# When GpSimd may refill a ring of gathered rows: released by the products that read them, or by the whole first layer behind them

## The chip, the cores and the metric

The kernel runs on one core of one Trainium2 chip. The metric is device time in microseconds (us) of one execution. The names of the engines are those of the profile: PE is TensorE, whose weight loads are told apart as PEld; DVE is VectorE, ACT is ScalarE, POOL is GpSimd, and SP is SyncE, which here only issues DMAs.

## The reference, cut to what matters

The reference is a graph network with 3125 nodes, 50000 edges and four message passing steps. The edges come sorted by their target node.

```
edge_attr = swish(edge_attr_raw @ enc_W + enc_b)                  # 50000 x 128
for _ in range(4):
    e_in = concat([edge_attr, x[src], x[dst]])                    # 50000 x 384
    e_upd = layernorm(swish(e_in @ eW1 + eb1) @ eW2 + eb2) * eg + ebeta
    edge_attr = edge_attr + e_upd
    agg = segment_sum(edge_attr, dst)                             # 3125 x 128
    x = x + layernorm(swish(concat([x, agg]) @ nW1 + nb1) @ nW2 + nb2) * ng + nbeta
return layernorm(x0 + x)
```

## The kernel before, in words

The product of the node features with their two parts of the edge layer's weights is made once per step and node and kept in two tables in DRAM: `p_table` for sources, `q_table` for targets. A row of `p_table` has 512 half-precision numbers (256 hidden units, as a high and a low part). So x[src] @ eW1 becomes a gather of rows of `p_table`.

Edges are worked on in groups of 512 (four tiles of 128, `TPG = 4`); there are 98 groups (`G1`) in each of the 4 steps. The input's edges are sorted, so every engine's program takes the branch that calls the functions `fast_...`, and there the object `F1` of the class `Edge` with `wide = False` does the edges.

In the pass of group g, PE does in this order (`fast_pe`):
- `hidden(g)`: 4 products with the target rows (L1123); 16 products that add the gathered source rows, four for each tile (L1131), after which it increments the semaphore `src`; then the 6 products of the first layer with the edge's own state (L1139), after which it increments `h`.
- `turn(g + 2)`: 8 transposes (L1103), then the semaphore `transposed`.
- `output(g - 1)`: a bias product (L1150) and the 24 products of the second layer (L1155), then the semaphore `v`.
- `node_sums(g - 7)`: 8 products with the 0/1 matrix of the targets (L1171), then the semaphore `sum`.

ACT waits for `h` to apply Silu (L1242, L1243), copies the transposed state (L1269), and waits for `v` to square the result with a sum (L1257). DVE makes the low half of the activations (L1349), adds the group's sums to `agg` when `sum` has come (L1419), and does the rest of the layer norm.

The gathered rows lie in a ring of four buffers (`R = 4`). POOL does nothing else in an edge step than gather them: for each group four indirect DMAs (L1080), one for each tile. Before the four it waits until the buffer of the group four places back has been read: L1078, a wait on `src`. The first four groups of a step have no such wait. The rest of the order is fixed by the program text; there is no planner. SP's queue loads the state, the matrices and the target rows and stores the new state.

Of the kernel before, what the change touches and what calls it, by code (L numbers as in the profile page):

```python
# [44 lines left out]
R = 4  # L45
# [14 lines left out]
def build_program(nc, x_in, src_in, dst_in, attr_in, enc_W, enc_b, eW1, eb1, eW2, eb2, eg, ebeta,  # L60
                  nW1, nb1, nW2, nb2, ng, nbeta, out):
    ctx = ExitStack()
    with ctx:
# [610 lines left out]
        class Init:  # L674
# [180 lines left out]
            def pool(self, pool):  # L855
                S, here, count = self.S, self.here, self.count

                for g in here:
                    k = g % R
                    pool.wait_ge(S("hi"), count(g))  # L860
                    pool.tensor_tensor(st0[k][:, :, D:2 * D], e0[k].rearrange("p (t f) -> p t f", t=TPG),
                                       st0[k][:, :, 0:D], ALU.subtract).then_inc(S("lo"), 1)
# [62 lines left out]
        class Edge(Groups):  # L925
# [142 lines left out]
            def pool(self, pool, s):  # L1068

                S = self.S  # L1070
                if s and not self.wide:
                    for t in range(CH):
                        pool.wait_ge(ND(f"tab{t}"), 16 * NCH * s)

                def gather(g):
                    k = g % R
                    if g - R >= self.lo:
                        pool.wait_ge(S("src"), s * self.per_step + g - R + 1)  # L1078
                    for t in range(TPG):
                        pool.indirect_dma_start(  # L1080
                            out=rows[k][:, t, :], out_offset=None, in_=p_table,
                            in_offset=bass.IndirectOffsetOnAxis(ap=idx_all[:, g, t:t + 1], axis=0),
                        ).then_inc(self.rows_sem(g), 16)

                for g in range(self.lo, self.hi):
                    gather(g)
# [825 lines left out]
```

## Time and profile before

| | |
|---|---|
| device time, median of 3 runs | 3248.82 us (3248.39 to 3252.28) |
| span of the profiled execution, first to last instruction | 3309.1 us |
| PE busy | 2595.5 us (78%) |
| DVE busy | 2336.3 us (71%) |
| ACT busy | 2083.8 us (63%) |
| POOL busy | 1702.6 us (51%) |
| mean share of the 16 DMA engines, four edge stretches | 0.67, 0.67, 0.66, 0.55 |
| granted TensorE clock there | 1.00 |

Of the profiled execution no other time than its span is given; the span is 60.3 us above the median of the runs without a profile. Busy times are those of records; a matmul's end is modelled, and its start says when it was taken up. "Idle before" in square brackets is how long an engine stood still before the row, and after the arrow stands what ended that; "remote" means that a semaphore came at that moment at which no recorded instruction ended.

### The profile page before, as it was taken

How to read it: one execution, taken by the hardware profiler on the slowest of the kernel's cores; microseconds unless marked ns; L12 is line 12 of the kernel's file. 1: busy time of each engine (PE TensorE's matmuls, PEld its weight loads, DVE VectorE, ACT ScalarE, POOL GpSimd, SP SyncE). 2: the span in 40 equal slices, each digit the busy share in tenths (PEclk: the TensorE clock that was granted, in tenths of full speed). 3: DMA queues.
4: the chain of work that ended last, by engine and by line, in shares of the span. 5: the costliest groups of instructions: out<-in, count | busy, mean ns of one | idle time of the engine just before them, and what ended most of it. 6: DMA issues, size and time to landing. Idle time of an engine off the chain costs nothing.

```text
span 3309.1 us, 86038 instructions
## 1 busy us (share of the span) xinstructions
PE 2595.5 (78%) x28086; PEld 1911.6 (58%) x28086; DVE 2336.3 (71%) x6778; ACT 2083.8 (63%) x5559; POOL 1702.6 (51%) x1679
## 2 busy tenths in 40 slices
PE   3665888888887788888887788888888688888886
PEld 1332666666664566666665566666665466666664
DVE  6884677777784577777786477777776377777777
ACT  3774666666663566666664566666675466666674
POOL 2445566566531556665640666665540665666550
PEclk8656999999999899999999899999999899999998
DMA  4776566666644566666653566666663455555550
GB/s 129 249 248 205 171 196 194 195 200 195 194 149 134 159 194 195 202 196 194 198 166 121 155 198 199 196 195 201 194 182 111 146 158 156 163 156 161 159 149 25
DMA packets 492918, 578.05 MB, mean 175 GB/s; under 512 B 82399, under 2 KB 341724, under 8 KB 492446
## 3 DMA queue, kind: packets, MB, share of 16 engines
q1 hardware_dynamic: 417198, 366.82, 34.8%
q0 software_dynamic: 75264, 205.62, 23.0%
q8 instruction: 228, 3.74, 0.5%
q14 instruction: 228, 1.87, 0.2%
HBM read 428.62 MB, written 144.35 MB: 173 GB/s over the span
## 4 chain that ended last, share of the span: by engine, by line
PE 59%; issue 16%; ACT 6%; DVE 6%; another core or an unknown queue 6%; DMA 3%; SPq 1%; DVEq 1%; POOL 0%; ACTq 0%; POOLq 0%
PE psum L1155 13%; PE psum L1139 13%; PE psum L1131 12%; PE psum L1123 5%; PE psum L1103 5%; PE psum L1171 4%; PE psum L1150 2%; PE psum L1577 2%; PE psum L1616 2%; ACT arena L1269 1%; ACT psum L1243 1%; ACT arena L1257 1%; PE psum L1590 1%; DMA arena<-attr_p 1%
## 5 line engine op out<-in xcount | busy, mean ns | idle before, releaser
L1080 POOL DMA_INDIRECT arena<-node_tables,idx_all x1568 | 1582.0, 1009 | 1342.0 <-PE psum L1131 626.5
L1257 ACT ACTIVATE arena<-psum 128x128 f32<-128x128 f32 x1568 | 411.6, 278 | 741.3 <-remote 723.1
L1131 PE MATMUL psum<-ident,arena 128*128 128x128 f16 x6272 | 548.1, 220 | 410.6 <-issue 398.8
L1131 PEld LDWEIGHTS psum<-ident,arena 128*128 128x128 f16 x6272 | 399.3, 98 | 541.1 <-issue 521.9
L1349 DVE SCALAR_TENSOR_TENSOR arena<-psum,arena 128x1024 f16<-128x1024 f32 x392 | 477.0, 1217 | 202.9 <-issue 146.9
L1155 PE MATMUL psum<-w_hi,arena 128*128 128x128 f16 x6272 | 595.2, 220 | 4.6 <-DVE arena L1349 3.5
L1155 PE MATMUL psum<-w_lo,arena 128*128 128x128 f16 x3136 | 550.5, 220 | 1.2 <-issue 1.2
L1419 DVE TENSOR_TENSOR agg<-agg,psum 128x128 f32 x392 | 113.0, 288 | 569.5 <-remote 544.8
L1242 ACT ACTIVATE arena<-psum 128x1024 f16<-128x1024 f32 x392 | 402.2, 1026 | 172.3 <-remote 75.7
L1155 PEld LDWEIGHTS psum<-w_hi,arena 128*128 128x128 f16 x6272 | 502.2, 98 | 6.8 <-DVE arena L1349 4.7
L1139 PE MATMUL psum<-arena,w_hi 128*128 128x512 f16 x1568 | 479.7, 386 | 29.8 <-issue 29.6
L1385 DVE SCALAR_TENSOR_TENSOR arena<-arena 128x128 f32<-128x128 f32 x1568 | 489.9, 346 | 4.0 <-DVE arena L288 0.4
L1269 ACT COPY arena<-psum 128x1024 f16<-128x1024 f16 x392 | 400.0, 1020 | 45.7 <-remote 22.0
L1243 ACT ACTIVATE psum<-psum 128x1024 f32<-128x1024 f32 x392 | 401.2, 1023 | 0.0
L1155 PEld LDWEIGHTS psum<-w_lo,arena 128*128 128x128 f16 x3136 | 308.8, 98 | 48.3 <-issue 3.5
L1257 ACT ACTIVATION_READ_ACCUMULATOR arena<-psum 128x1 f32 x1568 | 325.8, 208 | 0.0
L1139 PE MATMUL psum<-arena,w_lo 128*128 128x512 f16 x784 | 303.1, 387 | 7.8 <-issue 7.6
L1103 PEld LDWEIGHTS psum<-ident,arena 128*128 128x128 f16 x3136 | 211.5, 100 | 144.1 <-issue 46.6
L1359 DVE TENSOR_TENSOR arena<-psum,g_row 128x512 f32<-128x512 f32 x392 | 266.3, 679 | 30.3 <-ACT arena L1257 27.5
L1396 DVE SCALAR_TENSOR_TENSOR arena<-arena 128x512 f32<-128x512 f32 x392 | 279.2, 712 | 6.7
L1123 PE MATMUL psum<-arena 128*128 128x256 fp8e4 x1568 | 253.0, 274 | 36.3 <-issue 23.2
L1103 PE MATMUL psum<-ident,arena 128*128 128x128 f16 x3136 | 245.5, 222 | 41.4 <-DMA arena<-state 18.2
(172 smaller groups left out, 3514.9 us busy)
## 6 DMA issues: line engine op xcount, KB each, us to landing
state<-arena SPq DMA_DIRECT2D x392, 256.0 KB, 3.8
arena<-state SPq DMA_DIRECT2D x392, 256.0 KB
arena<-matrices SPq DMA_DIRECT2D x784, 64.0 KB
arena<-node_tables SPq DMA_DIRECT2D x784, 64.0 KB
node_tables<-arena SPq DMA_DIRECT2D x100, 256.0 KB, 2.4
arena<-node_tables,idx_all POOLq DMA_INDIRECT x1568
arena<-rel_rows SPq DMA_DIRECT2D x98, 128.0 KB, 3.9
matrices<-arena SPq DMA_DIRECT2D x98, 128.0 KB, 3.6
```

What stands on the lines that cost most here:

```text
L1080: pool.indirect_dma_start(out=rows[k][:, t, :], out_offset=None, in_=p_table, in_offset=bass.IndirectOffsetOnAxis(ap=idx_all[:, g, t:t + 1 ...
L1103: x = pe.transpose(ps_t[:, n * P:(n + 1) * P], st_in[k8][:, t, p * D:(p + 1) * D], ident16[:, :])
L1123: pe.matmul(ps_h(k2)[:, half, :].rearrange("q (t p) -> q t p", t=TPG)[:, :, h * HALF_N:(h + 1) * HALF_N], q_win[k][:, h * H + half * D:h * ...
L1131: x = pe.matmul(ps_h(k2)[:, half, t * P:(t + 1) * P], rows[k][:, t, p * H + half * D:p * H + half * D + D], ident16[:, :], start=False, st ...
L1139: x = pe.matmul(ps_h(k2)[:, half, :], w[:, cols], eT[k2][:, p, :], start=False, stop=w is w1_lo, skip_group_check=True)
L1155: x = pe.matmul(ps_v(k2)[:, t * P:(t + 1) * P], h[k2][:, half, t * P:(t + 1) * P], w[:, half, :], start=False, stop=half == 1 and h is hl, ...
L1242: act.activation(hh[k2], ps_h(k2), ACT.Silu).then_inc(S("hh"), 1)
L1243: act.activation(ps_h(k2), ps_h(k2), ACT.Silu).then_inc(S("h32"), 1)
L1257: x = act.activation(sq[k2][:, t * P:(t + 1) * P], ps_v(k2)[:, t * P:(t + 1) * P], ACT.Square, accum_out=nv[pair][:, n:n + 1])
L1269: act.copy(eT[k2].rearrange("p k e -> p (k e)"), ps_t[:, :]).then_inc(S("eT"), 1)
L1349: dve.scalar_tensor_tensor(hl[k2], ps_h(k2), 1.0, hh[k2], ALU.mult, ALU.subtract).then_inc(S("hl"), 1)
L1385: x = dve.scalar_tensor_tensor(e_new[k][:, t * P:(t + 1) * P], gu[k][:, t * P:(t + 1) * P], rs[pair][:, n:n + 1], st_in[k8][:, t, D:2 * D] ...
```

## The change

In `gather(g)` the wait keeps its value and its place and gets another semaphore, where `wide` is False, so in the sorted edge steps. It is now `h`, which PE increments after the first layer's products of group g - 4, in place of `src`.

```
                 def gather(g):
                     k = g % R
                     if g - R >= self.lo:
-                        pool.wait_ge(S("src"), s * self.per_step + g - R + 1)
+                        pool.wait_ge(S("src" if self.wide else "h"), s * self.per_step + g - R + 1)
                     for t in range(TPG):
                         pool.indirect_dma_start(
```

The order of instructions is the same on all engines. What is another is the wait ahead of four of POOL's gathers. On POOL, where the first edge step begins, there stands before (x3 means three more like it):

```order
982 L1080 DMA arena<-node_tables,idx_all 128x512 x15
983 L1080 DMA arena<-node_tables,idx_all 128x512 [waits edge_src]
984 L1080 DMA arena<-node_tables,idx_all 128x512 x3
985 L1080 DMA arena<-node_tables,idx_all 128x512 [waits edge_src]
986 L1080 DMA arena<-node_tables,idx_all 128x512 x3
```

and now:

```order
982 L1080 DMA arena<-node_tables,idx_all 128x512 x15
983 L1080 DMA arena<-node_tables,idx_all 128x512 [waits edge_h]
984 L1080 DMA arena<-node_tables,idx_all 128x512 x3
985 L1080 DMA arena<-node_tables,idx_all 128x512 [waits edge_h]
986 L1080 DMA arena<-node_tables,idx_all 128x512 x3
```

Each group's four gathers are released by another semaphore, 93 or 94 times in a step; nothing stands before or behind them that was not there.

On PE, the place between the two semaphores, the same before and now: `src` comes with the last of the 15 products of L1131 and `h` with the last of L1139.

```order
6500 L1131 MATMUL psum<-ident,arena 128x128 x15
6501 L1139 MATMUL psum<-arena,w_hi 128x512 [waits edge_eT]
6502 L1139 MATMUL psum<-arena,w_hi 128x512
6503 L1139 MATMUL psum<-arena,w_lo 128x512
6504 L1139 MATMUL psum<-arena,w_hi 128x512 x2
6505 L1139 MATMUL psum<-arena,w_lo 128x512
6506 L1103 MATMUL psum<-ident,arena 128x128 [waits edge_eT,edge_st6]
```

So six products of 512 columns and one wait (for the transposed state, `eT`) lie between the old release and the new one.

## Rows read from the trace of the kernel before

**Rows 1.** The page's costliest groups: line engine op names xcount | busy, mean ns | idle before, releaser.

```profile
L1080 POOL DMA_INDIRECT arena<-node_tables,idx_all x1568 | 1582.0, 1009 | 1342.0 <-PE psum L1131 626.5
L1257 ACT ACTIVATE arena<-psum 128x128 f32<-128x128 f32 x1568 | 411.6, 278 | 741.3 <-remote 723.1
L1131 PE MATMUL psum<-ident,arena 128*128 128x128 f16 x6272 | 548.1, 220 | 410.6 <-issue 398.8
```

**Rows 2.** Waits of the whole span: who <- for whom: us, times, longest us.

```profile
PEld psum L1131 <- DMA arena<-node_tables,idx_all: 9.8, 3, 3.6
```

**Rows 3.** Windows, instructions of L1131 alone: us, PE busy (x) PEld busy (x), clock, DMA.

```profile
400.00:900.00 500.00, 103.81 (x1184) 74.35 (x1184) 1.00 0.67 196
```

**Rows 4.** Timeline, one period mid-step: start us, us, engine line op names xcount [idle before].

```profile
602.36 0.94 POOL L1080 DMA_INDIRECT arena<-node_tables,idx_all  x1 [1.85 <-PE psum L1131]
...
603.00 0.38 PE L1139 MATMUL psum<-arena,w_lo 128*128 128x512 f16 x1
...
605.22 0.61 PE L1171 MATMUL psum<-arena 128*128 128x128 fp8e4 x8
...
606.13 0.22 PE L1131 MATMUL psum<-ident,arena 128*128 128x128 f16 x1
...
606.25 0.95 POOL L1080 DMA_INDIRECT arena<-node_tables,idx_all  x1 [0.31 <-issue]
...
606.67 0.38 PE L1131 MATMUL psum<-ident,arena 128*128 128x128 f16 x4 [0.32 <-issue]
...
608.15 0.72 PE L1131 MATMUL psum<-ident,arena 128*128 128x128 f16 x10 [0.49 <-issue]
608.30 0.28 ACT L1257 ACTIVATE arena<-psum 128x128 f32<-128x128 f32 x1 [2.00 <-remote]
...
609.15 1.20 POOL L1080 DMA_INDIRECT arena<-node_tables,idx_all  x1 [1.96 <-PE psum L1131]
...
609.79 0.38 PE L1139 MATMUL psum<-arena,w_lo 128*128 128x512 f16 x1
```

**Rows 5.** Timeline, the last groups of a step, whose gathers are all done.

```profile
958.59 0.38 PE L1139 MATMUL psum<-arena,w_lo 128*128 128x512 f16 x1
...
961.69 1.06 PE L1131 MATMUL psum<-ident,arena 128*128 128x128 f16 x16
961.77 0.29 ACT L1257 ACTIVATE arena<-psum 128x128 f32<-128x128 f32 x1
...
963.66 0.38 PE L1139 MATMUL psum<-arena,w_lo 128*128 128x512 f16 x1
```

**Rows 6.** Timeline, a period early in the second step.

```profile
1150.78 0.38 PE L1139 MATMUL psum<-arena,w_lo 128*128 128x512 f16 x1
...
1151.29 0.94 POOL L1080 DMA_INDIRECT arena<-node_tables,idx_all  x1 [1.18 <-PE psum L1131]
...
1155.67 0.33 PE L1131 MATMUL psum<-ident,arena 128*128 128x128 f16 x3 [1.21 <-issue]
...
1157.12 0.67 PE L1131 MATMUL psum<-ident,arena 128*128 128x128 f16 x9 [0.49 <-issue]
...
1158.70 0.38 PE L1139 MATMUL psum<-arena,w_lo 128*128 128x512 f16 x1
```

**Rows 7.** Timeline, a period early in the first step.

```profile
366.29 0.38 PE L1139 MATMUL psum<-arena,w_lo 128*128 128x512 f16 x1
366.40 0.95 POOL L1080 DMA_INDIRECT arena<-node_tables,idx_all  x1 [1.54 <-remote]
...
373.49 0.38 PE L1139 MATMUL psum<-arena,w_lo 128*128 128x512 f16 x1
```

**Rows 8.** Timeline, one disturbed period in the middle of the first step.

```profile
486.62 0.38 PE L1139 MATMUL psum<-arena,w_lo 128*128 128x512 f16 x1
...
487.39 0.94 POOL L1080 DMA_INDIRECT arena<-node_tables,idx_all  x1 [1.06 <-PE psum L1131]
...
495.10 0.63 PE L1139 MATMUL psum<-arena,w_lo 128*128 128x512 f16 x1
```

More of the change, by code:

```diff
@@ L1077, in gather @@
                     if g - R >= self.lo:
-                        pool.wait_ge(S("src"), s * self.per_step + g - R + 1)
+                        pool.wait_ge(S("src" if self.wide else "h"), s * self.per_step + g - R + 1)
                     for t in range(TPG):
```

## Prediction

> **What bounds the kernel now.** I started with the page's costliest groups [rows 1], because the change touches one wait of POOL. POOL has 1568 gathers, which is 392 groups of four, and it stands idle 626.5 us until a source-row product of PE (L1131) has ended: it is not short of time, it waits for PE. The next question is whether PE waits for POOL. By the view of all waits it hardly does: three times, 9.8 us in all [rows 2]. By data, then, POOL is far ahead: the gathers start when the pass four groups earlier has read its rows, and are read themselves four periods later, some 27 us (4 x 6.76, below), of which they need 5 and a landing. If that were all, a release that comes six products later would cost nothing.
>
> But the same rows show something that data does not explain. PE's products of L1131 stand idle 398.8 us until "issue", and ACT stands idle 723.1 us before L1257 until something "remote" [rows 1]. So I asked for the length of a period and for its rows in time. Between 400 and 900 us there are 1184 products of L1131, sixteen for each group, so 74 groups in 500 us: 6.76 us a group [rows 3]. At the end of a step, when no gather is left, the last product of the first layer starts at 958.59 and again at 963.66: 5.07 us a group for the same products (63.66 - 58.59), and the 16 of L1131 are one row of 1.06 us without a pause [rows 5]. There ACT's L1257 follows on at 961.77. So 1.69 us of each group's 6.76 are there only while POOL gathers.
>
> The period from 602.36 shows where they are [rows 4]. POOL's four gathers run from 602.36 to 607.20 (606.25 + 0.95): 4.84 us. PE gets through its first layer, transposes, second layer and sums without a pause, and from 606.13 on it issues the products of L1131 in driblets: one, four, one more (it is 16 in all; the row of the sixth is not shown), and ten from 608.15, when the gathers have been over for 0.95 us. The second layer's products were issued before 605.22, but ACT, which waits for them, starts at 608.30, after 2.00 us of idleness. The increments of PE arrive as if held until about a microsecond behind the last gather. Then the ten products run (0.72 us), `src` comes, and POOL starts the next four at 609.15, 0.28 us after 608.87. The period is thus a closed loop: 4.84 of gathers, 0.95 until PE runs freely, 0.72 of products, 0.28 of release, 6.79 in all. It is POOL's gathers, through the stall they cause in PE, and not PE's own work, that set the pace.
>
> **The change part by part.** Nothing is removed or added; one release moves from the last of L1131 to the last of L1139. Without a stall that is 1.30 us later (608.87 to 609.79 + 0.38 = 610.17) [rows 4]. As a delay of the gathers' data it costs nothing: the ring's slack of more than 20 us covers it. SP's waits, and everything on DVE and ACT, keep their semaphores. What is queued behind POOL's wait is only gathers.
>
> In the loop it is different. The release now needs ten or so products of L1131 *and* the six of L1139 once PE runs freely, and in return PE has done 1.30 us more of its pass when the gathers start. If PE could use that advance, nothing would change. The question is whether the advance survives the stall. The trace has periods in which the gathers happened to start at about the end of L1139, which is where the change puts them all:
> - Gathers at 1151.29, the last of L1139 ended at 1151.16 (1150.78 + 0.38), so 0.13 us behind it. PE stops sooner in time and at much the same place: three products of L1131 after a pause of 1.21, and nine still left at 1157.12. The next L1139 ends at 1159.08: 7.79 us after the gathers' start [rows 6].
> - Gathers at 366.40, 0.27 ahead of the end of L1139 (366.67); the next one ends at 373.87: 7.47 us [rows 7].
> - Gathers at 487.39, 0.39 behind the end of L1139 (487.00); the next ends at 495.73: 8.34 us. The last product there takes 0.63 in place of 0.38 us, so this period ran partly at TensorE's lower speed [rows 8].
>
> So the advance is lost: PE halts at about the same product, and what is left then is longer by the six products of the first layer. Adding the release (0.28) gives periods of 7.75, 8.07 and 8.62 us where the release is on `h`. The change puts the start 0.28 behind L1139, between [rows 6] and [rows 8]; I take 7.9, the mean of the two rows that ran at full speed throughout, and keep 7.75 and 8.62 as ends. Against 6.76 that is 1.14 us more for a group.
>
> How many groups: 392, less 16 (the first four of each of four steps have no wait), less some 28 (the first seven behind these in each step, in which PE has no sums of L1171 to do and a shorter pass) are 348. 348 x 1.14 = 397 us. The 28 I leave at nothing; at the same price they would add 32. The start of a step, where twenty gathers run back to back, may gain or lose a few us, since the fifth group's gathers now leave a gap; nothing for that either. The profiled span of 3309.1 would become 3706. The runs without a profile are 60.3 us shorter, so their period is at most 0.16 us shorter (60.3 / 376) and the loop must be there too; on their median 3248.8 + 397 = 3646 us.
>
> The Trainium skill has a rule that speaks against all this. The page "SBUF — State Buffer", section "SBUF: two separate sides", says that engine ports and DMA ports are disjoint, that neither can slow the other, and that PE and ACT never wait for anyone's port. By that, no placing of the gathers could hold up PE, and the sum would be nothing: 3249 us. The trace does not agree as far as the whole effect goes: 6.76 against 5.07 us with the same work on PE [rows 3, 5]. But what is held may be signals and not data, of which the page says nothing.
>
> **The rivals.**
> 1. *The data slack decides, no change.* The gathers' place in time does not matter, because the 1.69 us come from whatever the gathers cost in sum, or because in runs without a profile PE does not halt and only its signals are held to the gathers' end. Then `src` and `h` are both let go about a microsecond after the last gather, and the release is later by 0 to 0.1 us: 3249 to 3285. For it: what I read as driblets is read in a profiled execution, and ACT's wait shows that signals are held by themselves. Against it: with signals alone held the period would be 4.84 + 0.95 + 0.28 plus some 0.1 to 0.2, so 6.2 to 6.3, and 376 x 0.5 = 188 us would be missing between span and median, not 60.
> 2. *Faster.* With the start moved behind the first layer, the transposes and most of the second layer fall into the first gather, and their signals escape the hold; PE then gets through L1131 and L1139 before the fourth gather jams it. The period would be gathers, hold and release, 6.3 us: 376 x 0.46 = 173 us less, 3076. For it: in [rows 4] PE runs without a pause for the first 3.8 us of the gathers (602.36 to 606.13), so the hold does not begin with them. Against it: in [rows 6] the gathers start just so, and PE halts in L1131 all the same. It decides if PE can issue some 60 products between the gathers' start and its halt; in [rows 4] it is about 50.
> 3. *Slower, and more so.* The longer halts drop TensorE to its lower speed as in [rows 8], and the period goes to 8.62: 348 x 1.86 = 647 us, 3896.
>
> **How the numbers follow.** The forecast, with a period of 7.4 to 8.3, has 0.68; its own range is 3470 to 3785 (348 x 0.64 to 348 x 1.54). The third rival has 0.09, a smaller slowdown between 3285 and 3470 has 0.07, the first rival 0.08, and faster 0.08. Of the first rival half lies within 0.2% (6.5 us, about what a measurement of this kernel can tell from no change) and half is slower. So slower 0.88, same 0.04, faster 0.08. The range that leaves a tenth on either side is 3265 to 3790.
>
> **What would show it.** In the profile of the changed kernel: POOL's wait before L1080 ends on L1139 and its sum over the span rises from some 630 us to over 1000; products of L1131 in a stretch of 500 us fall from 1184 to about 1010 (500 / 7.9 x 16); PE still halts inside L1131 or just before it, with six to ten of its products and all of L1139 behind the hold's end; the groups without gathers at a step's end keep 5.07 us; waits of PE for gathered rows stay near nothing. The prediction is wrong if PE passes L1131 and L1139 before it halts (then the period is 6.3 and the kernel is not slower), or if a period's length no longer is the gathers' 4.84 us plus what PE does after them.

## The result, and the profile after

The changed kernel takes 3329.74 us (median of 4 runs, 3323.17 to 3348.15); the kernel before took 3250.55 us on the same chip (3248.39 to 3254.11, 4 runs). The ratio is 1.0247, 95% interval 1.0229 to 1.0266. The forecast was 3646 us: slower is right, and the size is wrong by five times, +79 us for +397. The time lies below the forecast's own range of 3470 to 3785, in the band of a smaller slowdown, to which I had given 0.07. The profiled execution after spans 3326.2 us.

The costliest groups of the page after answer to [rows 1]:

```profile
L1080 POOL DMA_INDIRECT arena<-node_tables,idx_all x1568 | 1597.5, 1019 | 1340.9 <-PE psum L1139 583.9
L1257 ACT ACTIVATE arena<-psum 128x128 f32<-128x128 f32 x1568 | 414.3, 283 | 634.3 <-remote 604.7
L1131 PE MATMUL psum<-ident,arena 128*128 128x128 f16 x6272 | 490.8, 220 | 173.5 <-issue 164.2
```

The wait has moved to L1139, as the edit says, and POOL's idle time is 1340.9 us for 1342.0 in [rows 1]. But the trace of [rows 1] spans 3309.1 us; the second trace of the kernel before, at the medians (e1, below), has 1264.9. Against that one POOL idles 76.0 us more, which is the measured difference but for 3 us, and its gathers are no longer (1597.5 for 1600.2 us busy). PE's pauses inside L1131 have about halved (164.2 us for 309.5 in e1 and 398.8 in [rows 1]), where the forecast wanted them kept. The view of all waits shows where they are now (who <- for whom: us, times, longest us):

```profile
POOL arena L1080 <- PE psum L1139: 583.9, 324, 5.9
...
PEld psum L1139 <- issue: 243.9, 424, 2.7
...
PEld psum L1103 <- DMA arena<-state: 171.2, 136, 3.3
...
PEld psum L1131 <- DMA arena<-node_tables,idx_all: 7.9, 2, 4.7
```

The weight loads of L1139 wait 243.9 us (before 74.7 us in 108 waits, in e1 99.8 in 183), so PE often halts in the first layer now. The wait of the transposes of L1103 for their state rows has grown from 7.2 us in 6 waits (13.1 in 17 in e1). Data of the gathers is still never late [rows 2]. The products of L1131 in 400 to 900 us answer to [rows 3], and contradict the forecast of about 1010:

```profile
400.00:900.00 500.00, 94.05 (x1197) 75.11 (x1198) 1.00 0.67 197
```

One period of the timeline after in which PE is caught (start us, us, engine line op, names, xcount, idle before), beside [rows 4]:

```profile
585.57 1.06 POOL L1080 DMA_INDIRECT arena<-node_tables,idx_all  x1 [2.68 <-PE psum L1139]
...
588.02 0.63 PE L1131 MATMUL psum<-ident,arena 128*128 128x128 f16 x8
...
589.06 0.38 PE L1131 MATMUL psum<-ident,arena 128*128 128x128 f16 x4 [0.41 <-issue]
...
589.44 0.94 POOL L1080 DMA_INDIRECT arena<-node_tables,idx_all  x1 [0.30 <-issue]
...
591.26 0.23 PE L1131 MATMUL psum<-ident,arena 128*128 128x128 f16 x1 [0.50 <-issue]
...
591.32 0.28 ACT L1257 ACTIVATE arena<-psum 128x128 f32<-128x128 f32 x1 [3.10 <-remote]
591.32 0.59 PE L1139 MATMUL psum<-arena,w_hi 128*128 128x512 f16 x2
...
592.40 0.38 PE L1139 MATMUL psum<-arena,w_lo 128*128 128x512 f16 x1
...
593.05 1.00 POOL L1080 DMA_INDIRECT arena<-node_tables,idx_all  x1 [2.66 <-PE psum L1139]
```

That is the mechanism of the forecast. The four gathers, which I call a burst from the first start to the last end, last 4.81 us (590.38 - 585.57), and PE is held until 591.32, which is 0.94 later (the last product of L1131 starts just before), with all six products of L1139 still to do (1.46, to 592.78). The release takes 0.27, and the period is 7.48 us. But the very next period is another one:

```profile
594.36 1.40 POOL L1080 DMA_INDIRECT arena<-node_tables,idx_all  x1 [0.30 <-issue]
...
595.50 0.78 PE L1131 MATMUL psum<-ident,arena 128*128 128x128 f16 x11
...
596.59 0.45 PE L1131 MATMUL psum<-ident,arena 128*128 128x128 f16 x5 [0.31 <-issue]
...
597.32 0.95 POOL L1080 DMA_INDIRECT arena<-node_tables,idx_all  x1 [0.30 <-issue]
...
597.55 0.38 PE L1139 MATMUL psum<-arena,w_lo 128*128 128x512 f16 x1
...
598.26 0.38 PE L1139 MATMUL psum<-arena,w_lo 128*128 128x512 f16 x1
...
598.97 0.62 PE L1103 MATMUL psum<-ident,arena 128*128 128x128 f16 x8 [0.33 <-DMA arena<-state]
...
599.38 1.46 POOL L1080 DMA_INDIRECT arena<-node_tables,idx_all  x1 [1.11 <-PE psum L1139]
```

Here the second gather took 1.40 us, the burst lasted 5.22 (593.05 to 598.27), and PE had issued L1131 and all of L1139 by the time it ended: 598.26 + 0.38 is 598.64. Nothing is owed, and the next burst starts 1.11 us behind the last gather: 6.33 us, less than any period I had quoted. The wait for state rows ends at 598.97, between PE's last product and POOL's release; it sits in the gap that the release sets anyway.

At the end of a step, without gathers, the pace is what it was in [rows 5], 60.43 - 55.36 = 5.07 us:

```profile
955.36 0.38 PE L1139 MATMUL psum<-arena,w_lo 128*128 128x512 f16 x1
...
960.43 0.38 PE L1139 MATMUL psum<-arena,w_lo 128*128 128x512 f16 x1
```

To count the two kinds I took, in each trace, the starts of the first gather of every group, groups 12 to 95 of each step (336 periods), and sorted them by length. "Before (again)" is e1 and "after (again)" is f1, both below:

```
kernel, release       mean   under 6.55    6.55-6.9     over 6.9
before (first)        6.72   17% at 6.49   75% at 6.74   8% at 7.02
before (again)        6.56   52% at 6.42   44% at 6.69   3% at 6.98
after                 6.77   55% at 6.40   16% at 6.74  29% at 7.46
after (again)         6.73   57% at 6.39   15% at 6.69  28% at 7.43
```

Against the second trace of before the change costs 0.21 us a group, times 376 groups 79 us, which is the measured difference; the two spans differ by 72.3 us. The second trace is the fair partner: it spans 3253.9 us, at the medians, and the one that I forecast from, 3309.1 us, was an untypical execution.

The length goes with what PE still owes when it is let go. I counted the products of L1131 and L1139 that start more than 0.45 us behind the last gather's end and before the next burst:

```
after        groups  nothing owed  one of L1139   2 to 6 of L1139  six and some of L1131
under 6.55     183        130           53               -                  -
6.55 to 6.9     54          1            8              45                  -
over 6.9        99          -            -              62                 37
```

With the limit anywhere from 0.3 to 0.7 us the last row stays, and the groups that owe nothing are 125 to 159. In the mean PE owes 0.3 products of L1131 and 2.1 of L1139 after the change (0.3 and 1.9 in f1), where before it owed 8.0 of L1131 (5.7 in e1) and had L1139 behind them. So even in the groups over 6.9 us, which I call caught, PE mostly halts inside L1139 and not in L1131.

### The profile page after: what moved, and what is told of

It reads as the page before. It is cut to its first block, busy times and chain, and to the rows that moved or that the text cites. A ratio compares the mean times of both kernels' runs of the same rounds, so it can differ in the third digit from the quotient of the medians.

```text
span 3326.2 us, 86038 instructions
## 1 busy us (share of the span) xinstructions
PE 2613.2 (79%) x28086; PEld 1904.2 (57%) x28086; DVE 2331.7 (70%) x6778; ACT 2069.3 (62%) x5559; POOL 1719.0 (52%) x1679
## 4 chain that ended last, share of the span: by engine, by line
DVE 25%; PE 24%; another core or an unknown queue 16%; issue 15%; ACT 9%; DMA 5%; DVEq 4%; SPq 2%; POOL 0%; ACTq 0%; POOLq 0%
DVE arena L1385 7%; PE psum L1139 5%; DVE arena L1349 5%; PE psum L1155 4%; DVE arena L1404 4%; PE psum L1131 3%; ACT psum L1243 3%; DMA arena<-state 3%; DVEq L1410 2%; DMA arena<-attr_p 2%; PE psum L1577 2%; ACT arena L1269 2%; ACT arena L1257 2%; PE psum L1171 2%
## 5 line engine op out<-in xcount | busy, mean ns | idle before, releaser
L1080 POOL DMA_INDIRECT arena<-node_tables,idx_all x1568 | 1597.5, 1019 | 1340.9 <-PE psum L1139 583.9
L1131 PE MATMUL psum<-ident,arena 128*128 128x128 f16 x6272 | 490.8, 220 | 173.5 <-issue 164.2
L1349 DVE SCALAR_TENSOR_TENSOR arena<-psum,arena 128x1024 f16<-128x1024 f32 x392 | 476.3, 1215 | 179.2 <-issue 125.7
L1139 PE MATMUL psum<-arena,w_hi 128*128 128x512 f16 x1568 | 495.3, 388 | 79.5 <-issue 76.5
L1131 PEld LDWEIGHTS psum<-ident,arena 128*128 128x128 f16 x6272 | 396.7, 98 | 225.6 <-issue 204.6
L1385 DVE SCALAR_TENSOR_TENSOR arena<-arena 128x128 f32<-128x128 f32 x1568 | 490.2, 346 | 4.2 <-DVE arena L288 0.4
L1103 PE MATMUL psum<-ident,arena 128*128 128x128 f16 x3136 | 256.8, 224 | 176.2 <-DMA arena<-state 114.5
L1103 PEld LDWEIGHTS psum<-ident,arena 128*128 128x128 f16 x3136 | 203.6, 100 | 323.0 <-DMA arena<-state 171.2
L1257 ACT ACTIVATION_READ_ACCUMULATOR arena<-psum 128x1 f32 x1568 | 333.3, 213 | 0.0
L1139 PE MATMUL psum<-arena,w_lo 128*128 128x512 f16 x784 | 305.6, 390 | 32.7 <-issue 28.9
L1359 DVE TENSOR_TENSOR arena<-psum,g_row 128x512 f32<-128x512 f32 x392 | 266.6, 680 | 30.0 <-ACT arena L1257 21.0
L1396 DVE SCALAR_TENSOR_TENSOR arena<-arena 128x512 f32<-128x512 f32 x392 | 276.4, 705 | 6.7
L1171 PE MATMUL psum<-arena 128*128 128x128 fp8e4 x3136 | 239.2, 219 | 45.0 <-DVE arena L1404 39.4
```

The costliest lines, as they stand in the source:

```text
L1080: pool.indirect_dma_start(out=rows[k][:, t, :], out_offset=None, in_=p_table, in_offset=bass.IndirectOffsetOnAxis(ap=idx_all[:, g, t:t + 1 ...
L1103: x = pe.transpose(ps_t[:, n * P:(n + 1) * P], st_in[k8][:, t, p * D:(p + 1) * D], ident16[:, :])
L1131: x = pe.matmul(ps_h(k2)[:, half, t * P:(t + 1) * P], rows[k][:, t, p * H + half * D:p * H + half * D + D], ident16[:, :], start=False, st ...
L1139: x = pe.matmul(ps_h(k2)[:, half, :], w[:, cols], eT[k2][:, p, :], start=False, stop=w is w1_lo, skip_group_check=True)
L1171: x = pe.matmul(ps_a[:, 0:P], st_out[k][:, t, p * D:(p + 1) * D], oh[k][:, t * P:(t + 1) * P], start=t == 0 and p == 0, stop=t == TPG - 1 ...
L1257: x = act.activation(sq[k2][:, t * P:(t + 1) * P], ps_v(k2)[:, t * P:(t + 1) * P], ACT.Square, accum_out=nv[pair][:, n:n + 1])
```

## The experiments

They fell into six series, one chip each, always with the kernel before beside them. In three of them (the result's, the first and the third below) the kernel before takes 3250 to 3254 us. In the other three it takes 2721, 2735 and 2731 us; it has no trace there, but in those of its variants (e5, below) TensorE is not held. I call them holding and free series. Chip 5 of the record is holding in the third series and free in the fifth, so it does not go by the chip's number alone; what it goes by is open.

**First series (holding; before 3254.34 us).**

e1, the kernel before once more, no edit.

> The kernel before, unchanged, for a second profile: its first profiled execution had a span of 3309.1 us, 59 us over the median of its timed runs (3250.6). Theory 'loop' (a group's period is the gathers' 4.84 us, plus about 1 us until PE runs freely, plus what PE still owes to the release, plus 0.28 us): if a profiled execution is like the timed ones, the span is about 3249 us, the products of L1131 are about 1210 in 500 us in place of 1184 (period 6.6), and more groups pass with little of L1131 left behind the gathers. Rival 'a profile adds 60 us': the span is about 3309 us again and the timed runs stay at 3250.

3255.42 us, 1 to 0.9998 (0.9985 to 1.001). The page of this run beside [rows 1], and its window beside [rows 3]:

```profile
L1080 POOL DMA_INDIRECT arena<-node_tables,idx_all x1568 | 1600.2, 1021 | 1264.9 <-PE psum L1131 540.8
L1257 ACT ACTIVATE arena<-psum 128x128 f32<-128x128 f32 x1568 | 413.0, 279 | 707.5 <-remote 684.1
L1131 PE MATMUL psum<-ident,arena 128*128 128x128 f16 x6272 | 529.5, 220 | 319.2 <-issue 309.5
```

```profile
400.00:900.00 500.00, 102.50 (x1213) 76.04 (x1211) 0.99 0.68 201
```

1213 products for 1184, as the theory said: half of the groups in a typical execution go at 6.4 us, a mode that my first trace showed in 17% of them.

e2, gathers for the first four groups of each step alone:

```
-                for g in range(self.lo, self.hi):
+                for g in range(self.lo, self.hi if self.wide else R):
```

> Leaves out all gathers of source rows but those of the first four groups of each step (the rows read later are old ones, so that part of the computation is left out); all PE, ACT, DVE and SP work stays. Theory 'loop': the 1.5 to 1.7 us a group above 5.07 us come from the gathers, so 376 groups lose 1.5 each: 2650 to 2720 us, 16 products of L1131 in one piece, no remote waits of ACT before L1257. Rival 'other work sets the pace' (ACT, DVE, state loads): at most 100 us less, 3150 to 3250.

2693.6 us, ratio 0.8271 (0.8247 to 0.8295): as expected, the gathers cost this kernel 561 us here. The source rows of all later groups are stale.

e3, release by the transposes two groups back:

```
-    pool.wait_ge(S("src"), s * self.per_step + g - R + 1)
+    pool.wait_ge(S("transposed"), s * self.per_step + g - R + 3)
```

> POOL's wait is moved a further 0.45 us down PE's pass, to the eight transposes behind the first layer (semaphore transposed of group g - 2). Theory 'loop, what PE owes at the end of the hold': the release needs the transposes too, so each group that got through in the change pays up to 0.45 us more and each that halted pays it too: 3330 + 376 x 0.3 to 0.45 = 3440 to 3500 us. Rival 'phase alone' (the later start is what costs or helps, and PE's halt moves with it): 3330 us or less, since the first gather then covers still more of the second layer.

3308.86 us, 1.0168 (1.014 to 1.0197). The theory missed: a release still later than that of the change costs less than it.

e4, two and two: the third and fourth gather also wait for the second layer's products of five groups back.

```
     for t in range(TPG):
+        if t == 2 and not self.wide and g - R - 1 >= self.lo:
+            pool.wait_ge(S("v"), s * self.per_step + g - R)
```

> The same gathers and the wait on src as before, but the last two of a group's four gathers wait for the second layer's products of that pass (semaphore v of group g - 5), some 3.3 us behind src. Theory 'a row of four gathers back to back is what jams PE': two bursts of 2.2 us leave a gap in which the hold ends, PE halts seldom, period 5.1 to 5.6: 2780 to 2950 us. Rival 'each gather costs PE the same wherever it stands': 3250 us. Rival 'v is itself held, so the second pair comes a hold later': slower than before, 3300 to 3600 us.

3177.07 us, 0.9758 (0.9737 to 0.9779): faster than both kernels, by much less than expected. All 336 periods but one are under 6.55 us, 6.36 in the mean. Its timeline shows the price of a pair:

```profile
601.68 0.94 POOL L1082 DMA_INDIRECT arena<-node_tables,idx_all  x1 [0.90 <-remote]
...
602.94 1.08 POOL L1082 DMA_INDIRECT arena<-node_tables,idx_all  x1 [0.32 <-issue]
...
604.85 0.94 POOL L1082 DMA_INDIRECT arena<-node_tables,idx_all  x1 [0.83 <-remote]
...
606.10 0.95 POOL L1082 DMA_INDIRECT arena<-node_tables,idx_all  x1 [0.31 <-issue]
...
608.05 0.94 POOL L1082 DMA_INDIRECT arena<-node_tables,idx_all  x1 [1.00 <-remote]
```

Each pair waits 0.83 to 1.00 us behind the pair before it. So the delay of a signal behind the last gather is paid for two gathers as for four. That the split wins because PE owes nothing long when it is let go is argued and not shown.

**Second series (free; before 2721.09 us).** Meant to vary the release and the burst.

e5, release on the third of the six products of L1139; e6, on the second layer's products of five groups back; e7, without the fourth gather of each group (stale rows there); e8, eight gathers behind one wait:

```
e5: +  if half == 0 and not self.wide: x.then_inc(S("mid"), 1)     and POOL waits for "mid"
e6: +  pool.wait_ge(S("v"), s * self.per_step + g - 5 + 1)
e7: +  for t in range(TPG if self.wide or g - R < self.lo else TPG - 1):
e8: +  elif g % 2 == 0: pool.wait_ge(S("src"), s * self.per_step + g - R + 2)
```

> POOL's wait stands between the kernel before and the change: on the third of the six products of L1139. Theory 'halts, priced by the products that PE still owes' (a floor of about 6.4 us a group for all; the groups in which PE halts pay the products left up to the release, and those of 512 columns cost 0.22 us each against 0.06 for the others): between the two, nearer to before, 3265 to 3300 us. Rival 'waiting on h as such' (the wait on eT in front of L1139, the end of the accumulation): 3250 us, since neither is in it. Rival 'phase alone': 3330 or more.

> POOL's wait moves still further down PE's pass, to the end of the second layer's products (semaphore v of group g - 5, some 3.3 us behind src). Theory 'halts, priced by what PE owes': the products in front of this release are of 128 columns and cost 0.056 us each, as in front of src, and the six dear ones lie early in the burst, where PE runs freely: about as before, 3230 to 3300 us, few groups over 6.9. Rival 'the later the release the slower': over 3330 us. Rival 'v is held like the others and adds a hold': 3500 us or more.

> As before, but the fourth gather of each group (but of the first four of a step) is left out, so a quarter of the source rows is old. Theory 'floor = burst plus a fixed 1.3 us': burst 3.7 + 1.3 = 5.0, so PE's own 5.07 becomes the bound, 5.1 to 5.3 us a group: 2700 to 2790 us. Rival 'each gather costs PE the same' (1.49 us a group in excess of 5.07, a quarter less): 6.2 us, 3110 us.

> Same gathers, but the wait on src stands before every second group only, so eight gathers run back to back and then POOL pauses once. Theory 'PE halts after some 50 products in a row of gathers and then gets a few in 0.6 us': 10 us of gathers, 1 us, and what PE then owes of its 134 products for two groups (40 to 50, 3 us): 14 to 15 us for two groups, 7.0 to 7.4 a group: 3400 to 3560 us. Rival 'the pause at the end of each burst is the cost, whatever its length': one pause for two groups, 5.6 a group: 2900 us.

They measured 2721.55 (1.0007, 0.9994 to 1.002), 2720.48 (0.9997, 0.9984 to 1.001), 2686.96 (0.9883, 0.9849 to 0.9917) and 2722.15 us (1.0002, 0.9985 to 1.0019). All expectations missed, for one reason, seen in e5's timeline:

```profile
602.05 0.95 POOL L1080 DMA_INDIRECT arena<-node_tables,idx_all  x1 [0.30 <-issue]
...
602.63 1.06 PE L1131 MATMUL psum<-ident,arena 128*128 128x128 f16 x16
602.71 0.28 ACT L1259 ACTIVATE arena<-psum 128x128 f32<-128x128 f32 x1
...
603.30 0.95 POOL L1080 DMA_INDIRECT arena<-node_tables,idx_all  x1 [0.30 <-issue]
```

PE issues its 16 products in one row while POOL gathers without end, ACT does not wait, and POOL is never released late (no idle time before a gather of a steady group but its own 0.3 us): the gathers, back to back, make 5.24 us a group, little over PE's own 5.07. That is why a quarter of the gathers less wins only 34 us in e7. The gather itself is no faster (1001 ns in the mean, 1009 in [rows 1]). Where nothing is held, the place of the release is worth nothing.

**Third series (holding; before 3253.59 us).** The change again, and the second series' kernels again.

> The changed kernel again, beside the kernel before on the same chip. On one chip so far the kernel before took 3254 us, on another 2721 us, where no signal of PE is held during the gathers. Theory 'the change costs only through the hold': where the kernel before takes some 3250 us, the change takes 3330 (2.5% more); where it takes some 2720, the gathers run back to back, POOL never waits for PE for long, and the change takes 2720 too (within 0.3%). Rival 'the later release costs in itself': 1% or more slower on either.

> POOL's wait on the third of the six products of L1139, as e5_rel_mid, whose chip did not hold signals. Where the kernel before takes 3250: theory 'halts, priced by what PE owes' 3265 to 3300 us; rival 'h as such' 3250; rival 'phase alone' 3330 or more. Where it takes 2720: 2720.

> POOL's wait on v of group g - 5, as e6_rel_v. Where the kernel before takes 3250: theory 'halts, priced by what PE owes' 3230 to 3300 us; rival 'the later the slower' over 3330; rival 'v adds a hold' 3500 or more. Where it takes 2720: 2720.

> Eight gathers back to back and one wait for two groups, as e8_pairs. Where the kernel before takes 3250: theory 'PE halts after some 50 products' 3400 to 3560 us; rival 'the pause is the cost' 2900. Where it takes 2720: 2720.

f1, the change: 3327.06 us, 1.0239 (1.021 to 1.0267), as expected. f2, release inside L1139: 3350.97, 1.029 (1.0265 to 1.0316), over 3265 to 3300 and dearer than the change itself. f3, release by the second layer: 3265.25, 1.0037 (1.0023 to 1.0051), as expected. f4, eight in a row: 4107.01, 1.2645 (1.2609 to 1.2681), far over 3400 to 3560. By place in PE's pass:

```
release                          ratio    under 6.55    6.55-6.9     over 6.9
L1131, source rows (before)      1.000    52% at 6.42   44% at 6.69   3% at 6.98
third of L1139 (f2)              1.029    23% at 6.37   31% at 6.80  46% at 7.08
L1139, first layer (change)      1.024    57% at 6.39   15% at 6.69  28% at 7.43
L1103, transposes (e3)           1.017    41% at 6.46   40% at 6.67  19% at 7.21
L1155, second layer (f3)         1.004    39% at 6.48   61% at 6.65   none
```

Time does not grow with the lateness of the release. It is worst where the 128x512 products of L1139 stand just before it and falls again behind them. A burst plus its hold, 6.4 to 6.5 us, is common to all; what differs is how often PE is caught in front of the release, and with how much. Why f2, with half of L1139 in front of its release, catches more groups than the change (46% over 6.9 us for 28%) the count does not say, and there the theory "priced by what PE owes" failed.

In f4 what PE owes grows with the burst, and the clock falls. Its costliest wait, its first-layer products and its clock (tenths, in 40 slices of the span):

```profile
POOL arena L1083 <- PE psum L1134: 1439.3, 188, 10.2
```

```profile
PEclk7568888888898888788898888888889788888888
...
L1142 PE MATMUL psum<-arena,w_hi 128*128 128x512 f16 x1568 | 593.5, 458 | 68.2 <-issue 65.3
```

Three windows of one period show both (us, busy us of PE, PEld, DVE, ACT and POOL, clock, DMA share, GB/s):

```profile
604.66:611.00 6.34, 2.20 (x21) 1.30 (x19) 1.71 (x3) 0.25 (x1) 4.80 (x5) 0.91 0.81 235
611.00:616.50 5.50, 5.31 (x27) 2.93 (x27) 3.61 (x16) 3.73 (x12) 0.00 (x0) 0.50 0.10 31
616.50:619.50 3.00, 3.00 (x47) 2.79 (x45) 2.86 (x8) 2.45 (x10) 0.00 (x0) 0.98 0.67 208
```

The eight gathers run from 600.97 to 610.97. From 604.66 on PE gets 21 products out in 6.34 us, and when it is let go it still has a whole pass in front of the release, some 70 products where the expectation had 40 to 50. It does the first of them at a granted clock of 0.50, the lower of the two levels, 1.2 GHz, and POOL goes on at 619.57. Over the run the product takes 458 ns for 388 after the change, and the mean granted clock is 0.822. The expectation has no term for that.

**Fourth and fifth series: a pause, and the split with the change.** Open was what lets PE pass L1139 before it halts. In the traces it goes with the length of the burst (the change, all 336 periods): bursts under 4.85 us leave 11% of the periods under 6.55, from 4.85 to 5.0 it is 26%, to 5.15 71%, above that 93%; in f1 it is 8, 39, 65 and 85%. So a pause inside the burst ought to make the change cheaper. (The "six second-layer products" in g1's expectation are the six of the first layer, L1139.)

```
g1 and h1 (with the change), g2 (without it):
+    if t == 2 and not self.wide:
+        pool.memset(pause[:, :], 0).then_inc(S("paused"), 1)
+        pool.wait_ge(S("paused"), s * self.per_step + g + 1)
g3 and h2: the change with e4's edit;   g4: e7's edit
```

> The changed kernel with a pause on GpSimd between the second and third gather of a group in the sorted steps: it fills a 128x256 table of its own and waits for that, by an estimate from its other fills 0.3 to 0.5 us. Theory: what makes a group dear after the change is that PE has not yet issued the six second-layer products when it halts, and it gets past them when the gathers last a little longer; so the pause brings most groups to gathers + 1.25 us, the groups over 6.9 us fall from 29% to under 10%, and the time is 3270 to 3330, no more than the changed kernel though GpSimd does more. Rival, the pause only adds to a loop through GpSimd: 3327 + 376 groups x 0.3 to 0.5 us = 3440 to 3515, with the share of dear groups as it was.

> The same pause in the kernel before (release by the source-row products). There few groups are dear (3% over 6.9 us), so the theory gives it nothing to win and the pause adds most of itself: 3330 to 3400. Rival, a pause gives PE's signals a way out and is free in itself: at or under 3254.

> The changed kernel with its four gathers in two pairs: the first two wait for the first layer's end of the group four back (as the change has it), the third and fourth also for the second layer's products of the group five back. Theory: the gathers no longer stand back to back, PE is held twice for shorter and gets past the products in time, so the change costs nothing more: 3165 to 3220, near the 3177 of the same split with the source-row release. Rival, what costs is that the release comes after the six products whatever the gathers do: 3177 + 75 = 3250 or more.

> The kernel before without the fourth gather of each group (after the first four groups of a step; its source rows are then stale), once more, for a chip on which the kernel before takes about 3250 us. Theory, a group lasts its gathers and 1.25 us more: 3.9 + 1.25 = 5.15 us, close to PE's own 5.07, so 2700 to 2830. Rival, only the gather's own time goes: 3254 - 376 x 0.95 = 2897.

> The changed kernel with the pause, once more, for a chip on which the kernel before takes about 3250 us; where it takes about 2730, PE is not held and the pause costs its own 0.35 us a group. Theory (PE gets past the six products when the gathers last longer): 3270 to 3330, groups over 6.9 us under 10%. Rival, the pause only adds: 3327 + 376 x 0.35 = 3460.

> The changed kernel with its gathers in two pairs, once more, for the same question. Theory: the split ends the hold at a shorter burst and the change costs nothing more: 3165 to 3220. Rival: the release behind the six products costs by itself: 3250 or more.

Both further series were free ones (before 2735.48 and 2730.72 us), the repeat included, and the question stays open. g1: 2867.57 us, 1.0478 (1.0433 to 1.0523); g2: 2859.01, 1.0444 (1.0412 to 1.0476); h1: 2871.21, 1.0513 (1.0487 to 1.0539). g3: 2735.16, 0.9996 (0.9979 to 1.0014); h2: 2727.02, 0.9987 (0.9974 to 1.0001); g4: 2696.04, 0.9853 (0.9815 to 0.989). What they do show: in a free series the pause costs 124 to 140 us, which is 0.33 to 0.37 us times 376, and the fill itself lasts 0.33 us in g1's trace; with the change and without it, it costs the same within the intervals; and the split gives nothing and takes nothing there.

## Why the forecast was wrong in size

*What bounds the kernel.* Right for the holding series. Without gathers the kernel takes 2693.6 us for 3254.34, and the loop of gathers, hold, owed products and release is seen in the rows after as in [rows 4].

*The Trainium skill's rule* ("SBUF — State Buffer", section "SBUF: two separate sides"), by which no gather could slow PE, I set aside. In a holding series the measurement is against that conclusion, 561 us of 3254 in all, though no run shows whether a port of SBUF has to do with it. In the free series the trace agrees with it: PE runs its 16 products in one row beside the gathers. What I could not know is that both are to be had.

*The loop after the change, for a group that is caught.* Right in kind, and high: 7.48 in the timeline and 7.43 to 7.46 in the mean, for 7.9. Summed up: 4.81 + 0.94 + 1.46 + 0.27. The 7.9 came from [rows 6, 7], in which nine and five products of L1131 started after the hold, beside the six of L1139. After the change 62 of the 99 caught groups owe none of L1131 (63 of 95 in f1), and only four owe four or more.

*"So the advance is lost: PE halts at about the same product", for all 348 groups.* This is the step that failed. After the change PE gets further before it halts. In 131 of 336 groups (146 in f1) it owes nothing behind the burst, and in 61 (59) the last product of L1139 alone; 55 to 57% of the groups last 6.40 us, and 28 to 29% are caught. The groups that owe nothing are the mechanism of my second rival, at nearly its 6.3 us, beside the forecast's in the others. The sum by the shares, against 6.56: 0.29 x 0.90 - 0.55 x 0.16 + 0.16 x 0.18 = 0.20 us, times 376 is 76 of the 79 us. This only takes the measured mean apart; it does not say why the shares are what they are.

*Why I did not see it.* I took the length of a caught period from [rows 6 to 8], where the gathers happened to start at L1139's end, and read them as what every group would do. Counted now over the same trace, eleven of its 336 steady groups start within 0.5 us of that end, and the next L1139 ends 7.09 to 9.73 us later in all eleven, so more of these rows would not have warned me. Eight of the eleven have short bursts, of 4.69 to 4.85 us, and after the change about 89% of the periods with bursts under 4.85 are over 6.55 us as well, while 180 of 336 bursts there are over 5.0 us. But the short bursts are not the whole of it. In e1's trace of the same kernel 42 groups start within 0.5 us of that end, 25 of them with bursts over 5.0 us, and in 23 of these 25 the next L1139 still ends 7.27 us later or more. Most of those start ahead of it. Of the groups that start up to 0.5 us behind it, where the change puts them, e1 has 17, and the next L1139 ends within 6.5 us in two of the six with bursts over 5.0 and in none of the eleven with shorter ones. After the change these are 103 of 111 and 30 of 98 (111 of 122 and 26 of 77 in f1). So with the same start and the same length of burst PE gets further in the changed kernel. Rows of the kernel before, however many, did not stand for the changed kernel, and what makes PE get further in it is open.

A hint stood in the rows: POOL's idle time before these starts is 1.18 and 1.06 us [rows 6, 8] for 1.85 and 1.96 in [rows 4], so the period before each had owed nothing behind its burst. My count for the second rival was off too: from the end of one L1139 to the end of the next PE has 67 products (8 + 1 + 24 + 8 + 4 + 16 + 6) and not "some 60", and I made a yes or no of what is a share. Last, the pace of before: [rows 3] have 6.76, where typical executions have 6.56 and half of their groups at 6.42. That did not make the forecast too high; from 6.56 it would have been 348 x 1.34 = 466 us more. The 60.3 us between span and median, which I used to argue that the loop must be there, also said that the trace was of an untypical execution.

*The first rival*, in which the place of the release does not matter: its outcome holds in the free series as far as they were measured (e5 and e6, 1.0007 and 0.9997; the split of the change, 0.9996 and 0.9987; the change with the pause against the pause alone, 2867.57 and 2859.01 us). The plain change was not run there.

*The third rival*, a lower clock: not in the change (0.941 granted, 0.942 in e1), but eight gathers in a row bring it (0.822).

*The signs.* POOL's wait ends on L1139: right. Its sum over 1000 us: wrong, 583.9. Products in the window about 1010: wrong, 1197. PE halted in or just before L1131 with all of L1139 behind it: right in 37 of the 99 caught groups, and with six to ten products of L1131 left in almost none. 5.07 us at a step's end and no wait for gathered rows: right.

What stays open is why PE gets further before it halts after the change, and why one group is caught and the next is not. The length of the burst goes with the latter, in both traces of the change. That it is the cause was not shown, since the runs with a pause came to free series. In f2 the same lengths go with 2, 17, 11 and 50%, so it is not the whole of it.

## What to carry to other kernels

A wait that "issue" or "remote" ends can be a stall that comes with something else, here the bursts of gathers, and taking the gathers out showed it (561 us). A release costs little where its producer owes nothing long when the burst ends (f3, +0.4%), and splitting the burst won 2.4% (e4). Rows of the kernel before that look like the changed kernel are not the changed kernel: here the same start and the same length of burst ended otherwise. So before you put the price of a few periods on every group, give a share and not one case, and keep a real chance for the case that the stall itself moves. Hold the profiled span against the median, since a trace that is 2% off may be of another mixture. An edit that lives on such a stall should be timed in more than one series: the change costs 2.4 to 2.5% in two holding ones, and in the free ones, where it was not run by itself, no other place of the release cost anything.

## What the runs showed of the hardware

- Gathers of GpSimd slow TensorE in some series and not in others: the same kernel takes 3250 to 3254 us in three series (2693.6 in one of them without most gathers) and 2721 to 2735 in three others, so 19 to 20% more, while a gather lasts about as long in either (1009 to 1021 ns in the mean before, after and in e1, and 1001 in e5). What sets the two kinds of series apart is not known.
- In the holding series the signals that POOL, ACT and DVE wait for come about a microsecond behind the last gather of a burst, whether it has two (0.83 to 1.00 us of POOL's wait in e4), or four (1.11 in the row at 599.38). Behind f4's eight gathers ACT went on after 1.55 us (612.52 against 610.97).
- A gather lasts longer beside some work of DVE. In the trace after, taking as beside what overlaps by more than 0.3 us, gathers beside L1396 and L1404 both take 1.26 us in the mean (68, every one over 1.0), those beside none of L1349, L1359, L1396 and L1404 0.96 (458, 9% over 1.0), and those beside L1349 alone, which reads PSUM and SBUF, 0.95 (355, 2%). The Trainium skill's "SBUF — State Buffer" tells in the same section of a "DVE blocks DMA" trap, in which GpSimd can't write descriptors while DVE, in a mode that takes two ports, holds the pair they share. The trace agrees as far as L1396 and L1404, beside which the gathers are longer, have both inputs in SBUF. But so has the shorter L1385, and gathers beside it alone take 0.98 us (189). Which mode these instructions ran in, and whether the port is the reason, no run here shows.
- The mean granted clock is 0.946 without gathers (e2), 0.942 with four in a row (e1) and 0.822 with eight (f4), where it is 0.50 from 611.00 to 616.50, behind 6.34 us in which PE was busy for 2.20.
